# Four graph layers on one core: x turned before loading, c from v's column, one region for the sums of both head halves, new tables of places

## What is computed

```python
# layer 0: 8 heads of 32, masked scores, then layer norm
scores = q @ k.T / sqrt(32); scores = where(adj + eye > 0, scores, -inf)
x = layernorm(x + softmax(scores) @ v @ Wo.T + bo) * gamma + beta
# layer 1: a weighted graph and a gate of two columns
a = x @ w_g[:256];  c = x @ w_g[256:]
scores = q @ k.T / sqrt(32) + a[:, None] + c[None, :] + b_g + log(adj + 1e-9)
x = x + softmax(scores) @ v
# layer 2: one head, logits from two columns
f = x @ W_fc + b_fc;  logits = (f @ w_q) + (f @ w_k).T + (1 - adj) * NEG
x = x + softmax(leaky_relu(logits)) @ f
# layer 3: as layer 0, but scores + log(clip(adj, 1e-8)) instead of the mask
```

## Time and profile before

| | |
|---|---|
| median of 3 runs | 1841.64 us |
| profiled execution: time, span | 1840.3 us, 1838.4 us |
| busy share of the span: PE, DVE, ACT, POOL | 94%, 81%, 66%, 69% |
| mean granted TensorE clock | 0.99 |
| one group of 32 items (from the chain of waits: a layer 0 projection starts at 567.41, its like at 1014.72) | 447.3 us |

### The profile page before, as it was taken

The page is one execution under the profiler, slowest core; times in us unless marked ns, Lnnn a source line. Parts: engine busy times, 40 slices in busy tenths (PEclk is TensorE's granted clock), DMA queues, the critical chain, the costliest instruction groups (busy, mean ns, idle before and its releaser), DMA issues.

```text
span 1838.4 us, 54870 instructions
## 1 busy us (share of the span) xinstructions
PE 1731.4 (94%) x23564; PEld 1321.4 (72%) x23564; DVE 1483.9 (81%) x3008; ACT 1214.8 (66%) x1894; POOL 1269.3 (69%) x903
## 2 busy tenths in 40 slices
PE   5999998899999999889999999989999999998996
PEld 4677776777777777677777777767777777767774
DVE  5899877777799977877789987787779998777775
ACT  3567765567777676456776777546777676754675
POOL 4443898288964489638895459945888446992788
PEclk8999999999999999999999999999999999999998
DMA  6100010001120000100221000010112100011011
GB/s 166 36 30 13 19 37 25 24 25 53 49 75 19 19 19 31 47 2 25 60 75 43 24 19 19 25 46 8 42 53 71 42 19 18 15 36 35 14 30 36
DMA packets 67734, 66.46 MB, mean 36 GB/s; under 512 B 6051, under 2 KB 67493, under 8 KB 67493
## 3 DMA queue, kind: packets, MB, share of 16 engines
q1 hardware_dynamic: 66388, 62.16, 11.3%
q10 hardware_dynamic: 1104, 0.79, 0.1%
HBM read 54.54 MB, written 8.39 MB: 34 GB/s over the span
## 4 chain that ended last, share of the span: by engine, by line
PE 77%; DVE 17%; ACT 2%; issue 1%; POOL 1%; SPq 1%; DMA 1%; DVEq 0%; POOLq 0%; ACTq 0%
PE gx L609 23%; PE od L747 17%; PE sc L714 17%; PE gx L760 6%; PE gx L634 3%; PE sc L708 3%; PE sc L720 3%; DVE ring L999 3%; PE gx L796 3%; DVE qk L950 2%; PE gx L727 2%; DVE lg L1043 2%; DVE negm L972 1%; DVE parts L972 1%; DVE parts L975 1%
## 5 line engine op out<-in xcount | busy, mean ns | idle before, releaser
L594 POOL TENSOR_TENSOR ring<-ring,adj_c 128x1024 f32<-128x1024 f32 x256 | 609.4, 2406 | 107.7 <-ACT ring L865 55.1
L714 PE MATMUL sc<-qk 32*128 32x256 f32 x9216 | 410.8, 294 | 11.0 <-ACT m_rows L853 4.4
L714 PEld LDWEIGHTS sc<-qk 32*128 32x128 f32 x9216 | 320.5, 184 | 109.3 <-issue 62.7
L850 ACT ACTIVATE aside<-sc 128x1024 f32<-128x1024 f32 x192 | 196.6, 1024 | 232.4 <-PE sc L714 152.7
L865 ACT ACTIVATE ring<-sc 128x1024 f32<-128x1024 f32 x256 | 248.4, 1023 | 29.8 <-PE sc L720 29.3
L569 POOL TENSOR_TENSOR xs<-xs,bo 128x512 f32<-128x512 f32 x96 | 128.3, 1337 | 182.7 <-DVE xt_lo L942 163.5
L747 PE MATMUL od<-ring,vf 128*32 128x256 f32 x3072 | 243.9, 389 | 3.1 <-POOL ring L594 3.1
L747 PE MATMUL od<-ring,ones_r 128*32 128x256 f32 x3072 | 236.7, 380 | 0.0
L972 DVE TENSOR_REDUCE parts<-sc 128x4 f32<-128x1024 f32 x128 | 155.8, 1217 | 50.2 <-PE sc L714 49.5
L999 DVE TENSOR_TENSOR ring<-ring,adj_c 128x1024 f32<-128x1024 f32 x128 | 177.6, 1429 | 0.0
L863 ACT ACTIVATE ring<-sc,vf 128x1024 f32<-128x1024 f32 x128 | 135.8, 1113 | 36.5 <-PE sc L720 36.4
(11 more groups left out here) (146 smaller groups left out, 4433.5 us busy)
## 6 DMA issues: line engine op xcount, KB each, us to landing
adj_c<-in_adj_t SPq DMA_DIRECT2D x96, 256.0 KB, 2.8
adj_r<-in_adj SPq DMA_DIRECT2D x64, 256.0 KB, 3.0
xs<-in_x SPq DMA_DIRECT2D x32, 256.0 KB, 3.1
out<-xs SPq DMA_DIRECT2D x32, 256.0 KB, 2.2
wo<-in_w_o SPq DMA_DIRECT2D x2, 256.0 KB
ring<-in_w_q ACTq DMA_DIRECT2D x1, 256.0 KB, 3.8
ring<-in_w_k ACTq DMA_DIRECT2D x1, 256.0 KB, 4.3
ring<-in_w_v ACTq DMA_DIRECT2D x1, 256.0 KB, 4.6
```

Source lines behind the costliest of these rows:

```text
L594: pool.tensor_tensor(part, part, adj_c[i.mi % 3][:, t, :].unsqueeze(1).to_broadcast([P, G, N]), ALU.mult).then_inc(weighted, 1)
L714: mm = pe.matmul(sc[:, g, t * N:(t + 1) * N], buf[rows, a, c, t * P:(t + 1) * P], buf[rows, b, c, :], start=(n == 0 and not masked), stop= ...
L850: act.activation(aside[:], sc[:, 0:2, :], ACT.Copy).then_inc(set_aside, 1)
```

## The change

Five things, and with them new numbers in every table.

1. **Layer 0, T.** The host passes x also transposed (`x_t`). SP loads it to `x_raw` (two buffers; new stage LT), ScalarE copies the high part from there, POOL subtracts the low part. TensorE and VectorE have no T in layer 0. Layers 1, 2 and 3 keep theirs.
2. **Layer 1, c.** The 6 matmuls, the weights `cr_hi`, `cr_lo` and VectorE's L957 go. POOL's O writes c's column of v and its remainder to `c_pad` (two instructions more), the new O of TensorE turns that with 2 matmuls, the new O of ScalarE writes `c_rows`.
3. **Sums.** `od0` holds the outputs of all eight heads, `od1` the sums of both halves: a matrix `halves` in place of ones sends the sums of the one half to 16 rows of each 32, those of the other to the other 16.
4. **N** is one stage per item, after A3. The first turn takes 256 columns, the reciprocal 16, the second turn and the product 512. A0 waits for the previous item's N; the other A wait for none.
5. **POOL's XB** in layer 0 waits for the load of x alone.

```diff
+GX_STAGES = {"O": "ca", "T": "x", ...
+                elif s == "T":                                   # POOL
+                    pool.wait_ge(xt_hi_set, i.k + 1)
+                    pool.tensor_tensor(xt_lo[i.k % 2][:], x_raw[i.i0 % 2][:], xt_hi[i.k % 2][:].bitcast(F32), ALU.subtract)\
+                        .then_inc(x0_lo_set, 1)
                 elif s == "O":
+                    gate_c = vf[i.mi % NVF][:, :, D + 1:D + 2].to_broadcast([P, T, G])
...
+                    pool.tensor_copy(pad[:, :, :, 0], gate_c).then_inc(c_hi_set, 1)
+                    pool.wait_ge(c_hi_set, i.i1 + 1)
+                    pool.tensor_tensor(pad[:, :, :, 1], gate_c, pad[:, :, :, 0].bitcast(F32), ALU.subtract).then_inc(c_pad_set, 1)
...
-                    if s == "P" and i.l == 1:
...
-                        project(gx_of("ca", i)[:, 0:N], [lambda h: cr_hi[:, h, :], lambda h: cr_lo[:, h, :]],
-                                [lambda h: xh[:, h, :], lambda h: xl[:, h, :]]).then_inc(gx_sem("ca", i), 1)
...
+                elif s == "O":                                   # TensorE
+                    pe.wait_ge(c_pad_set, i.i1 + 1)
+                    pe.wait_ge(*gx_emptied("ca", i))
+                    for n in range(T):
+                        mm = pe.matmul(gx_of("ca", i)[:, n * P:(n + 1) * P], c_pad[i.i1 % 2][:, n, :], ident_r[:], start=True, stop=True)
...
-                    if t == 0 and i.mi:
-                        pe.wait_ge(o_set, C * (i.mi - 1) + grp + 1)
+                    if c == 0 and i.mi:
+                        pe.wait_ge(o_set, i.mi)
...
-                            lhs = ones[:, 0:DH] if half else vf[i.mi % NVF][:, t, head * DH:(head + 1) * DH]
+                            lhs = halves[:, grp, :] if den else vf[i.mi % NVF][:, t, head * DH:(head + 1) * DH]
+                            cols = slice(0, N) if den else slice(grp * N, (grp + 1) * N)
...
+                    dve.wait_ge(av_done, i.mi + 1)
+                    dve.transpose(sums_t[:], od[1][:, 0:N]).then_inc(turned, 1)
...
+                    dve.reciprocal(rden8[:], sums_t[:, 0:N:DH // C]).then_inc(inverted, 1)
...
+                    dve.transpose(rden[:].rearrange("p c (b r) -> p c b r", r=DH), each).then_inc(rden_set, 1)
...
+                    dve.tensor_tensor(o_t[i.mi % 2][:], od[0][:].rearrange("p (c n) -> p c n", c=C), rden[:], ALU.mult).then_inc(o_set, 1)
```

Of the tables two lines, those that put N and the A of layer 1:

```diff
-    "N": {DVE: [14.184, 16.686]},
+    "N": {DVE: [15.736]},
-    "A": {PE: [13.219, 14.013, 15.503, 15.976]},
+    "A": {PE: [13.274, 14.202, 14.988, 15.114]},
```

More of the change, by code:

```diff
@@ L43 @@
 MHA_PLAN0 = {
[L44 to L58, removed]
+    "T": {ACTE: [-1.817], POOL: [-4.306]},
+    "Q": {PE: [0.638], ACTE: [0.311], DVE: [0.667]},
+    "P": {PE: [0.77], ACTE: [1.21], DVE: [1.201]},
+    "V": {PE: [3.264], ACTE: [2.977], DVE: [-1.908]},
+    "S": {PE: [3.408, 5.292], ACTE: [3.9, 5.505], DVE: [4.213, 5.665]},
+    "U": {DVE: [5.949]},
+    "M": {PE: [8.032], ACTE: [8.03]},
@@ L59 @@
+    "E": {PE: [8.693, 10.285], ACTE: [8.572, 10.233], POOL: [6.308, 6.532], DVE: [9.887, 11.686]},
+    "A": {PE: [12.817, 13.397, 13.908, 14.486]},
+    "N": {DVE: [16.461]},
+    "F": {PE: [18.473]},
+    "XB": {POOL: [7.237]},
+    "H": {DVE: [19.126]},
+    "LC": {SP: [-2.096]},
+    "PC": {POOL: [3.785]},
 }
 MHA_PLAN1 = {
[L61 to L64, removed]
@@ L77 @@
+    "N": {DVE: [15.736]},
+    "F": {PE: [18.56]},
+    "XB": {POOL: [3.639]},
+    "H": {DVE: [19.172]},
+    "LC": {SP: [-7.314]},
+    "PC": {POOL: [0.102]},
 }
 MHA_PLAN3 = {
[L79 to L93, removed]
+    "T": {PE: [-0.744], ACTE: [-0.572], DVE: [-0.189]},
+    "Q": {PE: [0.291], ACTE: [0.337], DVE: [0.748775]},
+    "P": {PE: [0.702], ACTE: [1.08177], DVE: [1.18477]},
+    "V": {PE: [5.677], ACTE: [6.228], DVE: [-12.925]},
@@ L94 @@
+    "S": {PE: [3.532, 5.66], ACTE: [3.94, 5.683], DVE: [4.042, 5.215]},
+    "U": {DVE: [6.389]},
+    "M": {PE: [8.094], ACTE: [8.181]},
+    "E": {PE: [8.644, 9.965], ACTE: [8.556, 10.719], POOL: [7.682, 10.273], DVE: [8.409, 10.046]},
+    "A": {PE: [12.825, 13.643, 14.948, 15.19]},
+    "N": {DVE: [15.6198]},
+    "F": {PE: [19.3069]},
+    "XB": {POOL: [-1.226]},
+    "H": {DVE: [19.825]},
+    "LC": {SP: [-3.266]},
+    "PC": {POOL: [5.461]},
 }
 LN_PLAN0 = {
-    "B": {DVE: [20.521]},
-    "Z": {ACTE: [21.887]},
@@ L109 @@
+    "LX": {SP: [-6.82]},
+    "LR": {SP: [-15.311]},
+    "PR": {POOL: [-3.261]},
 }
@@ L265, in gnn_stack @@
             assert run == sorted(run), (engine, group)
+    for slot in range(3):
+        for run in ([i.ar for s, i, c in order[SP] if s == "LR" and i.ar % 3 == slot], [i.mi for s, i, c in order[SP] if s == "LC" and i.mi % 3 == slot]):
+            assert run == sorted(run)
+    dve_place = {(stage, i.k, c): n for n, (stage, i, c) in enumerate(order[DVE])}
+    with_ln = [i for i in items if i.ln]
+    for one, other, run in (("Y", "B", with_ln), ("U", "S", mha)):
+        for n, i in enumerate(run[2:]):
+            assert dve_place[one, run[n].k, 0] < dve_place[other, i.k, 0], (one, other, i.k)
     with ExitStack() as ctx:
```

214 lines of the change are left out of this document (102 added, 112 removed).

## The result

The changed kernel takes **1868.1 us** (median of 4 runs) against 1841.0 for the one before on the same chip: ratio 1.0144 [1.0126, 1.0161]. It is 1.4% slower; 1820 was forecast, with a range up to 1843. Its profiled execution took 1867.9 us, span 1865.1.

The account below looks back on a forecast made before the run. TensorE's list was taken to set the pace inside layers, VectorE close behind in layer 0, GpSimd in layer 1. 1840.3 − 14.1 − 13 + 11 + 2.4 + 3.4 + 0.5 − 11 + 0.5 = 1820.0 us; range 1794 to 1843.

Parts of the forecast that it names:

- T of layer 0: Layer 0, TensorE: four transposes of 0.44 us go from each of 32 items, −14.1 us.
- N, 2.06 us: VectorE's normalisation, now one per item: 2.06 us from start to start, against 3.08 for two before; bounds 1.54 and 2.6.
- Layer 1, Q behind T behind N: Layer 1: Q waits 0.7 us for VectorE's xt_lo in 16 items, +11 us.
- c of layer 1: Layer 1, TensorE: six matmuls (0.70 us) go and two turns (0.3) come, −0.4 on 32 items, −13 us.
- The passage from layer 0 to layer 1: VectorE, late there, loses 2.8 us of work; 2.8 of TensorE's 4.36 idle us return, four times: −11 us.
- The start: Start of the run: SP issues one load more ahead of the weights, +0.5 us.
- The entry into GAT: Entry into GAT: one A0 and one G per group stand behind the longer N, +3.4 us.
- A0 in the first items of layer 1: First items of layer 1: A0 of two items per group waits, 4.36 against 4.6 us, 8 × 0.3 = +2.4 us.
- rival 2: Layer 1: GpSimd's list sets the pace at 15.84 us per item, +19 us, 1839 us; chance 0.08.
- Rival 3: Layer 0: GpSimd's subtraction blocks VectorE's mask, 0.6 us of each 1.34 passes on, +19 us, 1839 us; chance 0.10.

Follow-up runs that it names:

- e3: Changed kernel with GpSimd's last layer-norm step (Y) ahead of the padded c and gate (O) in layer 0's table: 1845.5 us, 1.0018 of the kernel before.
- e12: Changed kernel with the scores S0 of layer 1's first item computed twice, nothing else changed: 1856.5 us, 1.0072 of the kernel before.
- e1: Changed kernel with the adjacency row load moved behind the next item's plain load on SyncE's list: 1860.7 us, 1.0101 of the kernel before.
- e5: e3 with layer 0's second masking later on VectorE, so that layer 3's residual add H stands ahead of it: 1846.6 us, 1.003 of the kernel before.
- e10: e1 and e3 in one, plus repeated scores in layer 1 and mask additions in layer 0 as extra TensorE work: 1835.5 us, 0.996 of the kernel before.
- e6: e3 with layer 1's turn T ahead of A2 on TensorE, O on ScalarE and N on VectorE: 1883.6 us, 1.0237 of the kernel before.
- e11: e1 and e3 in one, with GpSimd's residual bias XB of layer 0 2.2 slots earlier: 1844.0 us, 1.0011 of the kernel before.

## Why the prediction was wrong

By its own steps, with what was measured:

- **T of layer 0, −14.1: right.** An item takes 17.07 us on the mean of three in the second group (592.9 − 541.7), forecast 17.1, before 17.53; 16.92 where nothing else holds it up (123.01 to 139.93 in the first).
- **N, 2.06 us: right.** From 252.97 to the next start at 255.10 it is 2.13 us:

```profile
252.97 0.45 DVE L1025 STREAM_TRANSPOSE sums_t<-od 128x256 f32<-128x256 f32 x1 [1.20 <-PE od L775]
253.46 0.25 DVE L1027 RECIPROCAL rden<-sums_t 128x16 f32<-128x16 f32 x1
253.74 0.71 DVE L1030 STREAM_TRANSPOSE rden<-rden 128x512 f32<-128x512 f32 x1
254.49 0.69 DVE L1032 TENSOR_TENSOR o_t<-od,rden 128x512 f32<-128x512 f32 x1
255.10 0.68 DVE L968 TENSOR_TENSOR xt_lo<-gx,xt_hi 128x512 fp32r<-128x512 f32 x1
```

- **Layer 1, Q behind T behind N: right in kind and near in size,** 0.52 us of idle time an item (forecast 0.7). **c of layer 1: taken up by its neighbours.** The six matmuls are 0.7 us and the two turns 0.28, as forecast. But I priced each stage by its own rows. Ahead of an A or a scores group the last turn takes 0.20 us to the next start where those inside take 0.11. F, which stood in one run with T, now stands ahead of an A, 0.59 us where it was 0.50; M stands ahead of S0, 0.34 for 0.27. T takes 0.73 for 0.53, since M behind it waits for ScalarE's `c_rows` (written until 253.69, M starts at 253.84; I had 0.1 us for this). Some 0.4 us an item, the same as the gain. Items of 15.6 were forecast; they take 15.88.
- **The passage from layer 0 to layer 1, −11: the step that failed.** It was "Of the 4.36 us of idle PE I give back 2.8". Measured per group: +3.4 us over four items that each had 0.47 us less to do, so 5.3 us lost instead of 2.8 won, 8 us a group and some 32 of the 48 by which the sum is off. The windows above divide it. The idle time did not go (4.98 us for 4.51; 1.7 was forecast), 3.3 us a group; the rest, some 5 us a group, is TensorE's work at the lower clock, for which the sum had no term. Both hang on an order that I had not read: I had counted DVE's work and not looked at POOL in this place, where O came ahead of Y. e3 put that one right and won 22.6 us; in the second group's passage it has 1.8 us less idle time and no fall of the clock. And I priced a wait at its own length. e12 shows that the fall behind it is the larger part: it added 4.8 us of work, left one of the two waits as it was, and still took 11.6 us off the run.
- **The start, +0.5: wrong.** The first F is 2.4 us late. I counted the extra load and not what it moved: the row load of item 3, which waits for its buffer, now stood ahead of the weights' loads on SP. e1 moved it back behind them and brought the first F to 84.8, 1.9 us ahead of the kernel before.
- **Layer 3 to layer 0: I had no step for it.** T was also a stage in the turn of the two `gx` buffers. Without it Q takes the buffer that F filled and waits for DVE's H behind a masking (2.4 us, then the clock): 2.3 us a group in the table. e5 shows that the order of the two does not mend it, since DVE is full there; e10 fills it.
- **The entry into GAT, +3.4: not seen.** The distance stays at 14.0 to 13.9 from layer 1's item 4 to its item 8. **A0 in the first items of layer 1, +2.4,** lies inside the passage and cannot be told apart there; no wait of an A for DVE stands among PE's waits.
- **What is left of the 48:** some 7 us from layer 3 to layer 0, some 7 in layer 1 (4 × 2.6 measured, 3.8 forecast with these two terms) and 2 at the start.

The rivals: rival 2 (POOL sets layer 1) did not come by itself, but e6 came up against it (6.3 us of waits for Y). Rival 3 has its mechanism in the passage rather than in the steady items: the masking took 4.35 us beside POOL, 2.35 without. The Trainium skill (SBUF — State Buffer, the section on who interferes with whom) says such a pair takes turns; e11 agrees, the masking shortened by 0.67 us where one addition was moved away, and shows that moving it is no gain by itself. None of my rivals contained the clock. The Trainium skill (TensorE: Matmul & The Clock Gate, on oscillation in real kernels) does say that matmuls behind a long wait run at the lower clock, and that this comes on top of the wait; its case is a kernel that waits for DMAs. The traces agree in kind, with 40 matmuls in 5 us at a clock of 0.50 against 84 at 1.00.

What stays open: e12 shows that the fall costs more than the wait, and e12 and e10 that filling the gap prevents it there, though it can then come at another place. Why the same 1.98 us gap brings it in e5 and not in e3 is not settled; the spread within one kernel (e3) says that an order alone does not decide it. The clock of a single trace is one draw, and the lines above are of one execution each. Nor were the parts of the change (layer 0's turns, c, N) run one at a time; their sizes above are read from the traces.

## What to carry to other kernels

Price a wait of TensorE not at its length alone: read the granted clock of the stretch behind it, and where the list is tight between two stages of a program, look at each engine's order there before the sum is made for the steady part. A stage that is removed also leaves the rotation of its buffers and the queues of its loads, and both move other waits. If a gap cannot be closed, computing something twice in it can be faster than waiting. And compare more than one execution: where the clock falls is not the same in each.
